# Layer 0's small attention computed by heads in 32-column tiles right behind layer 1's values, and VectorE's and ACT's steps around it moved

## What is computed

```
# layer 0: "linear" attention over channels, 8 heads of 32 channels, group norm over the sample
q = Wq y + bq ; k = Wk y + bk ; v = Wv x + bv
scores = q_h k_h^T / 16               # 32 x 32 for each head
out = softmax(scores) v_h ; o = Wo out + bo + x ; x1 = groupnorm(o) * gn_w + gn_b
# layer 1: attention of y with itself in chunks of 64 positions, 8 heads of 32
q, k, v = W_in y + b_in ; a = softmax(q k^T / sqrt(32) + mask) v
z = instance_norm((W_out a + b_out) * mask + x1)
```

## Time and profile before

| | before |
|---|---|
| median of 3 runs | 1587.32 us (1583.64 to 1589.57) |
| the profiled execution | 1583.99 us, of which 1582.2 us are the span of the instructions |
| PE busy | 1525.3 us, 96% of the span, 23308 matmuls |
| PE weight loads busy | 1293.0 us, 82% |
| DVE busy | 1337.0 us, 85% |
| ACT busy | 1103.6 us, 70% |
| POOL busy | 442.9 us, 28% |
| DMA traffic | 157.17 MB, mean 99 GB/s |

### The profile page before, as it was taken

One profiled execution on the slowest core, in us unless ns is written; L12 is line 12 of the kernel. 1 busy time (PEld: TensorE's weight loads), 2 busy tenths in 40 slices (PEclk: granted clock), 3 DMA queues, 4 the chain that ended last, 5 costly groups with the idle time before them and its releaser, 6 DMA issues.

```text
span 1582.2 us, 53120 instructions
## 1 busy us (share of the span) xinstructions
PE 1525.3 (96%) x23308; PEld 1293.0 (82%) x23308; DVE 1337.0 (85%) x2020; ACT 1103.6 (70%) x2052; POOL 442.9 (28%) x292
## 2 busy tenths in 40 slices
PE   8999999999999999999999999999999999999984
PEld 6888888888888888888888888888888888888873
DVE  5778889888898888979888898888988889798886
ACT  6667676777757768577676767777577685776853
POOL 1114133141321414124141331413314141241412
PEclk9999999999999999999999999999999999999997
DMA  6132331423323242241423414233242422414121
GB/s 250 49 101 76 109 120 43 140 82 115 108 76 120 69 141 82 95 128 42 150 87 98 129 38 148 82 115 108 67 130 69 141 82 92 131 42 148 35 69 67
DMA packets 96326, 157.17 MB, mean 99 GB/s; under 512 B 5344, under 2 KB 38240, under 8 KB 95968
## 3 DMA queue, kind: packets, MB, share of 16 engines
q1 hardware_dynamic: 96096, 153.78, 30.8%
HBM read 120.20 MB, written 33.55 MB: 97 GB/s over the span
## 4 chain that ended last, share of the span: by engine, by line
PE 69%; ACT 14%; DVE 14%; issue 3%; DMA 0%; POOL 0%; DVEq 0%; SPq 0%; POOLq 0%
PE pj_ps L282 31%; PE l_ps L282 12%; PE l_ps L382 7%; PE s_ps L297 6%; PE w_ps L308 5%; PE w_ps L326 4%; ACT prob L572 3%; DVE x_lo L723 3%; ACT s_ps L583 3%; ACT prob_t L567 2%; DVE a L819 2%; PE l_ps L400 2%; DVE row_sum L745 1%; DVE o_sb L866 1%; ACT o_sb L593 1%
## 5 line engine op out<-in xcount | busy, mean ns | idle before, releaser
L952 POOL TENSOR_TENSOR prob<-prob,row_inv 128x1024 f32<-128x1024 f32 x128 | 244.8, 1912 | 953.4 <-DVE row_inv L750 953.4
L603 ACT CAST att_hi<-w_ps 128x256 fp32r<-128x256 f32 x256 | 83.3, 381 | 217.8 <-PE w_ps L326 217.7
L282 PE MATMUL pj_ps<-y_hi,w_hi 128*128 128x512 f32 x512 | 207.9, 406 | 0.8 <-DVE y_lo L715 0.8
L282 PE MATMUL pj_ps<-y_lo,w_hi 128*128 128x512 f32 x512 | 202.1, 395 | 0.0
L282 PE MATMUL pj_ps<-y_hi,w_lo 128*128 128x512 f32 x512 | 202.1, 395 | 0.0
L745 DVE TENSOR_REDUCE row_sum<-prob 128x16 f32<-128x1024 f32 x128 | 154.9, 1210 | 47.4 <-ACT prob L572 47.4
L297 PEld LDWEIGHTS s_ps<-k_s,q_s 32*64 32x64 f32 x8192 | 130.8, 133 | 43.2 <-issue 35.2
L969 POOL TENSOR_TENSOR o_sb<-o_sb,u_sb 128x1024 f32<-128x1024 f32 x63 | 164.8, 2626 | 3.8 <-ACT o_sb L593 2.9
L723 DVE TENSOR_TENSOR x_lo<-x_raw,x_hi 128x1024 fp32r<-128x1024 f32 x64 | 104.7, 1636 | 70.3 <-ACT x_hi L545 68.9
L567 ACT COPY prob_t<-w_ps 128x512 f32<-128x512 f32 x256 | 152.1, 595 | 12.6 <-PE w_ps L308 12.5
L308 PE MATMUL w_ps<-cst,prob 128*128 128x128 f32 x1024 | 146.8, 274 | 13.3 <-DVE att_lo L757 12.3
(11 more groups left out here) (110 smaller groups left out, 3663.3 us busy)
## 6 DMA issues: line engine op xcount, KB each, us to landing
y_raw<-in_ctx SPq DMA_DIRECT2D x64, 512.0 KB, 4.9
yt_raw<-in_ctx_t SPq DMA_DIRECT2D x64, 512.0 KB, 4.6
x_raw<-in_x SPq DMA_DIRECT2D x64, 512.0 KB, 5.1
out_z<-o_sb SPq DMA_DIRECT2D x64, 512.0 KB, 3.6
mask_b<-in_mask SPq DMA_DIRECT2D x64, 256.0 KB, 3.9
u_sb<-in_w SPq DMA_DIRECT2D x2, 512.0 KB, 5.1
w_sb<-in_w SPq DMA_DIRECT2D x1, 1024.0 KB, 11.1
cst<-in_consts SPq DMA_DIRECT2D x1, 512.0 KB, 7.0
```

Of the source, the lines that this page charges most:

```text
L282: last = mm(dst, lhs, rhs, start=i == 0, stop=i == len(todo) - 1)
L952: nc.gpsimd.tensor_tensor(cut, cut, row_inv[:, u % 2, :].unsqueeze(2).to_broadcast([P, 2 * HEADS, CHUNK]), ALU.mult).then_inc(probs_done, 1)
```

## The change

Six things are changed.

1. The row of k's sums and the scores leave the slots' ends. A new function `layer0_scores` stands in slot 8 directly behind `values`. It computes only the 32 x 32 blocks on the diagonal, each as a matmul in a tile of 128 rows and 32 columns, four tiles next to each other: 16 matmuls for the row of sums (L402's two before) and 16 for the scores (L408's four before).
2. u0 is computed by `layer0_values` in slot 10 directly behind `values`, in tiles of 32 x 32: 8 matmuls of 256 columns in the place of L414's two.
3. `a0`, `v_row`, `bk_l` and `y_sum_b` have 32 columns a half in the place of 128 (256 for both), and the mask's addition (L790) is gone. `v_row` is made in slot 8 ahead of the scores' bias.
4. M (L420, L423) moves from slot 11 to slot 10. `layer0(n, s)` stands ahead of `wout` in a slot, so it is also moved ahead of slot 10's `wout`.
5. On DVE, M's split stays in slot 11 but moves ahead of `result` (L866). On ACT, u0's copy moves to the front of slot 10, behind `copy_att`, and the copy of G's lower part (L629) moves ahead of a `copy_pt` in slot 7.
6. The first `layer0_output` waits for `o_bias` only before its second bank, and ACT waits for it in `copy_output`.

```diff
-S_SPLIT_T, S_GRAM, S_HL, S_HLT, S_SUM, S_T1, S_SC, S_U, S_M, S_X, S_MX = 0, 1, 4, 5, 6, 7, 8, 10, 11, 11, 12
+S_SPLIT_T, S_GRAM, S_HL, S_HLT, S_SUM, S_T1, S_SC, S_U, S_M, S_X, S_MX = 0, 1, 4, 5, 6, 7, 8, 10, 10, 11, 12
...
+            def layer0_scores(n):
+                pe.wait_ge(y_sum_done, count(n, 1, 0))
+                pe.wait_ge(gram_done, count(n, 1, 0))
+                for i in range(HALVES):
+                    for k in range(HALVES):
+                        for h in range(4):
+                            o = i * P + DH * h
+                            mm(l0_ps[0][DH * h:DH * h + DH, P + i * DH:P + (i + 1) * DH], y_sum_b[:, k, :], w0_sb[:, K_W, k, o:o + DH],
+                               start=k == 0, stop=k == 1)
+                pe.wait_ge(t1_done, count(n, 1, 0))
+                for i in range(HALVES):
+                    for k in range(HALVES):
+                        for h in range(4):
+                            o = i * P + DH * h
+                            last = mm(l0_ps[0][DH * h:DH * h + DH, i * DH:(i + 1) * DH], w0_sb[:, Q_W, k, o:o + DH], t1[:, k, o:o + DH],
+                                      start=k == 0, stop=k == 1)
+                last.then_inc(sc0_ready, 1)
+
+            def layer0_values(n):
+                pe.wait_ge(a0_done, count(n, 1, 0))
+                for i in range(HALVES):
+                    for h in range(4):
+                        rows = slice(DH * h, DH * h + DH)
+                        last = mm(l0_ps[1][rows, i * E:(i + 1) * E], a0[rows, i, :], w0_sb[rows, O_W, i, :], start=True, stop=True)
+                last.then_inc(u0_ready, 1)
...
                 if q == 0:
                     pe.wait_ge(m_lo_done, count(n, 1, 0))
-                    pe.wait_ge(o_bias_done, count(n, 1, 0))
                 for o in range(HALVES):
+                    if q == 0 and o == 1:
+                        pe.wait_ge(o_bias_done, count(n, 1, 0))
...
+                    if s == S_SC:
+                        layer0_scores(n)
+                    if s == S_U:
+                        layer0_values(n)
...
+                    if s == S_U:
+                        copy_u0(n)
                     if not first and s in (4, 6):
                         group_normed(n - 1, s // 2)
+                    if s == S_SUM + 1:
+                        copy_lower(n)
                     if e == 1 and not (first and u == 0):
                         copy_pt(n, u - 1, 1)
...
-                    tt(a0[:, :, :], a0[:, :, :], head_mask.unsqueeze(1).to_broadcast([P, HALVES, P]), ALU.add).then_inc(a0_step, 1)
...
+                    if s == S_M + 1:
+                        layer0(n, s)
                     if not first and T_FINAL <= s < T_FINAL + BLOCKS:
                         result(n - 1, s - T_FINAL)
```

More of the change, by code:

```diff
@@ L111, in build @@
         gram = u0 = work_b
[L112 to L113 removed]
+        v_row = sb("v_row", [P, HALVES, DH])
+        a0 = sb("a0", [P, HALVES, DH])
         a0_max = sb("a0_max", [P, HALVES])
@@ L396, in layer0 @@
                     pe.wait_ge(gram_done, count(n, 1, 0))
-                    pe.wait_ge(y_sum_done, count(n, 1, 0))
                     for i in range(HALVES):
                         for k in range(HALVES):
-                            mm(l0_ps[1][:, i * E:(i + 1) * E], gram[:, k, i * P:(i + 1) * P], w0_sb[:, K_W, k, :], start=k == 0, stop=k == 1)
-                    for k in range(HALVES):
-                        last = mm(l0_ps[0][:, 0:E], y_sum_b[:, k, :], w0_sb[:, K_W, k, :], start=k == 0, stop=k == 1)
+                            last = mm(l0_ps[1][:, i * E:(i + 1) * E], gram[:, k, i * P:(i + 1) * P], w0_sb[:, K_W, k, :], start=k == 0, stop=k == 1)
                     last.then_inc(t1_ready, 1)
[L404 to L415, removed]
                 elif s == S_M:
@@ L615, in copy_output @@
                     act.wait_ge(stored[q], count(n - 1, 1, 0, 16))
+                if q == 0:
+                    act.wait_ge(o_bias_done, count(n, 1, 0))
                 for o in range(HALVES):
@@ L652, in _ @@
             act.wait_ge(w0_in, 2 * 16)
-            nc.scalar.mul(bk_l[:, :], bk_row[:, :], float(L)).then_inc(consts_done, 1)
+            for h in range(4):
+                rows = slice(DH * h, DH * h + DH)
+                last = nc.scalar.mul(bk_l[rows, :, :], bk_row[rows, :].rearrange("p (i o) -> p i o", i=HALVES)[:, :, rows], float(L))
+            last.then_inc(consts_done, 1)
             def body(n, first, last):
@@ L778, in layer0 @@
                     for i in range(HALVES):
-                        stt(out=t1[:, i, :], in0=bk_row[:, :], scalar=y_sum[:, i:i + 1], in1=l0_ps[1][:, i * E:(i + 1) * E],
-                            op0=ALU.mult, op1=ALU.add)
-                    tt(v_row[:, :], l0_ps[0][:, 0:E], bk_l[:, :], ALU.add).then_inc(t1_done, 1)
+                        last = stt(out=t1[:, i, :], in0=bk_row[:, :], scalar=y_sum[:, i:i + 1], in1=l0_ps[1][:, i * E:(i + 1) * E],
+                                   op0=ALU.mult, op1=ALU.add)
+                    last.then_inc(t1_done, 1)
                 elif s == S_SC:
                     dve.wait_ge(sc0_ready, count(n, 1, 0))
-                    dve.wait_ge(t1_done, count(n, 1, 0))
+                    tt(v_row[:, :, :], l0_ps[0][:, P:P + HALVES * DH].rearrange("p (i o) -> p i o", i=HALVES), bk_l[:, :, :],
+                       ALU.add).then_inc(a0_step, 1)
+                    dve.wait_ge(a0_step, count(n, 4, 0))
                     for i in range(HALVES):
-                        last = stt(out=a0[:, i, :], in0=v_row[:, i * P:(i + 1) * P], scalar=col[:, V_BQ0, i:i + 1],
-                                   in1=l0_ps[0][:, i * P:(i + 1) * P], op0=ALU.mult, op1=ALU.add)
+                        last = stt(out=a0[:, i, :], in0=v_row[:, i, :], scalar=col[:, V_BQ0, i:i + 1],
+                                   in1=l0_ps[0][:, i * DH:(i + 1) * DH], op0=ALU.mult, op1=ALU.add)
                     last.then_inc(a0_step, 1)
-                    dve.wait_ge(a0_step, count(n, 4, 0))
-                    tt(a0[:, :, :], a0[:, :, :], head_mask.unsqueeze(1).to_broadcast([P, HALVES, P]), ALU.add).then_inc(a0_step, 1)
                     dve.wait_ge(a0_step, count(n, 4, 1))
@@ L921, in body @@
                         layer0_normalize(n)
-                    layer0(n, s)
+                    if s != S_M + 1:
+                        layer0(n, s)
                     if s == SLOTS - 1 and not last:
```

14 lines of the change are left out of this document (5 added, 9 removed).

## The result

| | before | after |
|---|---|---|
| median of 7 runs each | 1585.26 us (1583.64 to 1589.57) | 1596.77 us (1592.10 to 1604.60) |
| the profiled execution | 1583.99 us, span 1582.2 | 1596.77 us, span 1594.7 |

The ratio is 1.0074, with a 95% interval of 1.0051 to 1.0097: the change made the kernel 0.7% slower. I had forecast no difference that can be measured.

A forecast was written before the change was run, and what follows sets the result against it. PE bounds the product-to-T1 stretch; from T1 to product PE and DVE are nearly full. Gains of 0.95 and 1.34 us, spent on waits of 0.35, 0.7 and 1.2, leave 0.05 a sample: 1586 us, range 1573 to 1604.

The forecast's parts named there:

- the term under "PE's work" for the 64 passes: Slot 8: the added sums and scores, 64 passes of 32 columns, cost PE 0.65 us a sample, between 0.55 and 1.1.
- The 64 small passes within 1.1 us: Sign to look for in the changed profile: slot 8's block of sums and scores lasts no more than 1.1 us.
- The clock: Rival: behind the 1.2 us wait before the product, passes at half pace cost 1.4 us a sample, 1608; chance 0.08.
- The wait in slot 7: Slot 7: without L402, PE waits 0.35 us before `wout` for the bank that DVE's `branch` frees.
- the time from `branch` to the product: Slots 11 to 12: the product with x starts 6.35 us behind the start of slot 11's `branch`.
- `x_lo` ahead of POOL: Behind slot 11's `branch`: DVE's `x_lo` starts some 0.1 us before POOL's multiplication; rival POOL first, 1601, chance 0.12.
- the cast held: Ahead of the product: DVE's cast to `m_hi` is held by POOL, about 1.3 us; rival not held, 1577, chance 0.18.
- the wait before the product: Slot 12: PE, ready at D + 5.15, waits 1.2 us for DVE before the first product with x.
- u0's wait: Slot 10: PE waits 0.7 us before u0, because DVE's division of a0 ends only at 841.25.
- the 0.86 that I took off: Slot 7: removing L402, four passes of 256 columns, takes 0.86 us a sample off PE.
- the earlier start of T1: Slot 7: ACT copies G's lower part earlier, so T1 starts 0.15 us sooner.
- Tiles in one bank: Rival, slot 10: u0's four tiles in one bank don't run at once; in pairs 1600, one by one 1627; chance 0.10.

The follow-up runs named there:

- the two shifted kernels: Changed kernel with PE's list lengthened once ahead of the first sample, by 128 instructions (1611.38 us) or by 64 (1602.13 us).
- the scores late: Changed kernel with the block of small sums and scores at the end of slot 8 instead of directly behind values: 1573.16 us, ratio 0.9934.
- the kernel with both edits: Changed kernel with M behind slot 10's output projection and the small sums and scores at the end of slot 8: 1556.67 us, ratio 0.9830.
- The same block: Kernel before plus 64 unread small passes in slot 8: directly behind values 1609.62 us, or between the transposes and `layer0` 1589.23 us.

## Why the prediction was wrong

**The step that failed** is the term under "PE's work" for the 64 passes: I priced the new block by its passes alone (0.65 us a sample) and had no term for what PE's program costs. The passes themselves took 0.70 from start to start, as forecast (447.98 to 448.68), but directly behind scores and values it made PE run dry: 17.6 us more of gaps (19.2 against 1.6). The measured 1596.77 lies between the 1573 and 1604 that I had named, but that is luck: the range was made of other rivals, and none of them happened in that form. "The 64 small passes within 1.1 us" held in samples 1 to 8, and not in 9 to 16, where a gap lies in the block. The kernel before had the sign of it, four gaps with no releaser of 0.3 to 0.6 us, two in values and two up to 2 us behind it, and 184 packets in the program's queue; I read neither.

**The clock.** I gave the fall 0.08 and tied it to the wait of 1.2 us before the product. It did not come there in any sample, but behind the gaps in slot 8, twice. The gap alone does not decide: with M behind the projection a gap of 1.87 us was followed by no fall, while in the two shifted kernels gaps of 1.56 to 1.64 us were followed by one. What else it takes is not shown. The two samples take 32.41 and 32.30; 28.57 (the same stretch with the scores late) and their gaps of 1.88 and 1.78 make 30.45 and 30.35. Samples 8 to 10 and 13 to 16, with gaps and no fall, are 0.4 to 0.5 over such a sum, so a fall costs about 1.6 us, 3.2 in all, by my estimate.

**The rest of the sum** was right in its mechanisms, and less so in its sizes. The wait in slot 7 (0.35 forecast, 0.40), the time from `branch` to the product (6.35, and 6.26 from 464.74 to 471.00), `x_lo` ahead of POOL, the cast held (1.3, 1.41), the wait before the product (1.2, 1.18) all came as worked out. u0's wait was 0.14 in the place of 0.7: a0 ended at 457.50 (456.26 + 1.24), 15.24 behind T1's start where I had 15.02, and PE was later there than I had it. One cause is L402: its four passes are worth 0.68 us between starts (828.06 to 828.74), not the 0.86 that I took off. The other 0.3 to 0.4 us of it I have not traced. Span for span, 12.5 us less 17.6 of gaps and 3.2 of clock is -8.3, half a microsecond a sample, where I had 0.05. Of it, 0.28 are between T1 and the product (29.02 to 28.74) and up to 0.35 between the product and the next T1 (67.01 to 66.66 in most samples), less what gaps leave behind them. For the second I had 0.15, the earlier start of T1, and for the first 0.10 more, not less, since the product was to move by 0.05 only. Why both came out better I have not traced.

**Held casts.** The Trainium skill, "SBUF — State Buffer", "Who interferes with whom", has the lock of VectorE's and GpSimd's shared ports. The runs agree: the cast took 1.41 us beside POOL and 0.43 without it.

**Tiles in one bank.** u0's 16 passes in four tiles of one bank take 0.99 us from start to start (829.91 to 830.90 in the kernel with both edits), as I had taken it; one by one they would take 3.5. So this rival is out, and here the rule of the Trainium skill's "TensorEngine Tiling (Array Packing)", "Gotcha 1: PSUM Pressure", does not hold as it is worded.

**Fetching.** The Trainium skill, "Runtime: NRT & Kernel Launch", "Instruction fetch mechanics", has an engine's program refilled in blocks of 16 KiB, 256 instructions, by a DMA queue of the sequencer's own, which agrees with the packets and with the 197 modulo 256. It also says that this is hidden, because instructions are issued more slowly than they arrive. That does not hold here, with 17 gaps and 19.2 us in the changed kernel.

**By size:** gaps +17.6, clock +3.2, the rest -8.3, together the 12.5 between the spans. The falls are counted by themselves because they need not follow from the gaps. Without the gaps and the falls the change would have been faster by 0.5%, and it was so where its block stood elsewhere (1573.16).

## What to carry over

Count instructions as well as microseconds: on PE each small matmul brings its weight load, and 256 instructions that run in well under the 2.8 to 3.6 us below can stall it, by up to 1.9 us in these runs, wherever a piece of the program ends in them. Don't set one burst of small matmuls directly behind another; put large ones between them. The same block cost 3.5 us there and 25 here; about half of the difference were gaps, and a third was a wait that it filled there. And a step that is moved ahead of a projection delays all that hangs on the projection: M's place alone was worth 17.7 us, 14.3 of them as one wait.

## What the runs showed of the hardware

- PE goes on from a gap 2.2 to 2.9 us after the start of the 16 KB packet; in the gap shown above the packet itself took 1.4 of them. In 15 of the 17 gaps the instruction 256 places earlier had run 2.8 to 3.6 us before PE goes on, so the packet starts behind it; in the other two it was 5.9 and 8.2 us. What exactly starts the packet stays open, since those two are not explained by it.
- The sum of the gaps hardly depends on the phase (19.2, 19.5 and 19.9 us for three shifts), but strongly on the burst's length (at the block and in values 15.9 us with 384 instructions in slot 8, 8.3 with 320). Each sum is that of one execution.
- A wait on a semaphore that is long there costs PE 98 ns.
- 32 passes of 32 columns in four column tiles take 0.28 us from start to start, 9 ns each.
